# Router of the last batch with buffers of its own, and final statistics spread over two experts

## The reference

```python
x = layernorm(x + retention(x) + conv5(x))        # scan over tokens, one 512x512 product, 5 taps
x = layernorm(x + mlstm(q=x, k=ctx, v=ctx))       # 8 heads of 64, gates, decay matrix D:
#   C = (q k^T / 8) * D ;  h = C v / (max(|sum C|, exp(-m)) + 1e-6) ;  h = layernorm(h) * ln_scale
x = layernorm(x + moe(x))                         # 32 experts, top 2, capacity 160, 16 shared adapters
# moe: router input = [x, mean, std, min, max, l2, share of |x| < 1e-6]  (512 + 6 features)
#   h = gelu(input @ r1_w.T + r1_b) ; probs = softmax(h @ r2_w.T) ; the two best experts of a token
#   each expert takes its 160 best tokens: silu(gate) * up, then down, scattered back with weights
```

## Time and profile before

| | |
|---|---|
| Time of three runs | 1695.46 us median (1693.04 to 1701.02) |
| The profiled execution: its own time, its span | 1692.79 us, 1691.0 us |
| Busy share: TensorE, VectorE, ScalarE, GpSimd | 87%, 56%, 27%, 18% |
| Drain, from the last step's head work to `save` | about 528 to 605 us of the span |
| Selection, then the experts | from 605 us; expert 31 begins at 1638 us |

### The profile page before, as it was taken

How to read it: one execution, slowest core, us unless ns; L and a number is a source line. 1 busy time by engine, 2 the same in 40 slices (tenths; PEclk the granted TensorE clock), 3 DMA queues, 4 the chain that set the end, 5 groups by cost and what they waited for, 6 DMA issues and landing times.

```text
span 1691.0 us, 29270 instructions
## 1 busy us (share of the span) xinstructions
PE 1474.4 (87%) x10885; PEld 1132.8 (67%) x10921; DVE 953.3 (56%) x2778; ACT 463.0 (27%) x1111; POOL 309.3 (18%) x399
## 2 busy tenths in 40 slices
PE   5679998898898720499999999999999999999995
PEld 3356555555556410388887878888787888878784
DVE  8667999999987879624233242423324242332463
ACT  4556576676654510010010100001010010101023
POOL 4002121121111100111211212121121212112134
PEclk9689999999998755599999999999999999999998
DMA  6213213223210261056767677676777767677796
GB/s 174 69 31 89 75 63 113 64 74 83 80 51 1 100 277 59 16 184 238 290 218 293 243 278 269 234 292 219 288 248 270 277 229 293 219 293 249 267 348 197
DMA packets 92575, 311.03 MB, mean 184 GB/s; under 512 B 42838, under 2 KB 46940, under 8 KB 83164
## 3 DMA queue, kind: packets, MB, share of 16 engines
q1 hardware_dynamic: 79260, 287.87, 46.5%
q0 software_dynamic: 13248, 22.29, 5.8%
HBM read 273.18 MB, written 36.96 MB: 183 GB/s over the span
## 4 chain that ended last, share of the span: by engine, by line
PE 69%; DVE 22%; issue 5%; ACT 3%; POOL 1%; DMA 1%; DVEq 0%; POOLq 0%; ACTq 0%
PE bank L1003 37%; PE banks L1017 14%; PE bank L634 6%; PE banks L1020 4%; DVE arena L1405 3%; DVE arena L1836 2%; DVE arena L1395 2%; PE bank L636 1%; PE banks L731 1%; DVE arena L1567 1%; DVE arena L1576 1%; PE banks L712 1%; DVE arena L1426 1%; DVE arena L1445 1%; DVE arena L1893 1%
## 5 line engine op out<-in xcount | busy, mean ns | idle before, releaser
L1340 ACT ACTIVATE arena<-bank 128x160 f32<-128x160 f32 x288 | 87.1, 303 | 947.3 <-PE bank L1003 947.3
L1003 PE MATMUL bank<-keep,arena 128*128 128x160 f32 x2304 | 319.4, 299 | 2.4 <-DVE arena L2018 2.4
L1003 PE MATMUL bank<-arena 128*128 128x160 f32 x2304 | 320.1, 301 | 0.8 <-issue 0.8
L1003 PEld LDWEIGHTS bank<-keep,arena 128*128 128x128 f32 x2304 | 315.3, 189 | 5.8 <-issue 3.2
L1003 PEld LDWEIGHTS bank<-arena 128*128 128x128 f32 x2304 | 316.3, 191 | 4.2 <-issue 4.2
L2018 DVE TENSOR_TENSOR arena<-arena,bank 128x160 f32<-128x160 f32 x256 | 82.1, 321 | 405.6 <-ACT arena L1340 405.6
L1017 PE MATMUL banks<-arena 128*128 128x512 f32 x576 | 252.4, 592 | 0.0
L2203 POOL DMA_INDIRECT acc_rows<-arena,keep x64 | 102.8, 1606 | 625.6 <-DVE arena L1963 609.3
L1017 PEld LDWEIGHTS banks<-arena 128*128 128x128 f32 x576 | 107.6, 190 | 122.5 <-issue 122.5
L1961 DVE TENSOR_SCALAR arena<-banks,keep 128x512 f32<-128x512 f32 x32 | 24.0, 750 | 189.2 <-PE banks L1020 185.5
L634 PE MATMUL bank<-arena 128*128 128x512 f32 x224 | 107.8, 626 | 7.0 <-DVE arena L1405 7.0
(11 more groups left out here) (280 smaller groups left out, 1775.3 us busy)
## 6 DMA issues: line engine op xcount, KB each, us to landing
arena<-in_wup SPq DMA_DIRECT2D x32, 4096.0 KB, 12.4
arena<-in_wdn SPq DMA_DIRECT2D x32, 2048.0 KB, 9.4
arena<-in_aup SPq DMA_DIRECT2D x32, 512.0 KB, 11.5
arena<-in_xT SPq DMA_DIRECT2D x32, 256.0 KB, 2.8
arena<-in_kT SPq DMA_DIRECT2D x8, 1024.0 KB, 5.5
arena<-in_v SPq DMA_DIRECT2D x32, 256.0 KB, 6.3
x_rows<-arena SPq DMA_DIRECT2D x8, 1024.0 KB, 4.5
acc_rows<-arena SPq DMA_DIRECT2D x8, 1024.0 KB, 6.9
```

The costliest lines, as they stand in the source:

```text
L1003: m = pe.matmul(u[:, g * CAP:(g + 1) * CAP], w, xeT[e.slot][:, c, :], start=(c == 0), stop=(c == C - 1))
L1340: act.activation(sg[k], Ub[k][:, 0:CAP], ACT.Silu).then_inc(up_a(f"silu{j}"), 1)
```

## The change

Batch b gets its own buffers for sums and statistics. In the drain, its odd score tiles go to `Pp`, its even value tiles to `Sp`, and the order of several pieces moves on ScalarE, VectorE and TensorE. In the last two experts, VectorE's statistics are divided differently, and GpSimd's fourth `shifts` moves behind the scatter of expert 30.

```diff
+        rsum_l, rsq_l, nz_l, rvar_l, rt_l = (room.take(TB) for _ in range(5))
+        st6_l = room.take(TB, NSTAT)
+        def sums(b):
+            return (rsum_l, rsq_l, nz_l, rvar_l, rt_l, st6_l) if b.off == NB - 1 else (rsum, rsq, nz, rvar, rt, st6)
...
         def value_banks(b, j):
-            return Sp if b.off == NB - 1 and j % 2 else Pp
+            return Sp if b.off == NB - 1 and j % 2 == 0 else Pp
+        def score_banks(b, j):
+            return Pp if b.off == NB - 1 and j % 2 else Sp
...
             def scores(b, j):                                   # TensorE
+                if j == 1 and b.off == NB - 1:
+                    pe.wait_ge(*ev_v.at(f"out{NP - 1}", b - 1))
+                elif j and b.off == NB - 1:
+                    pe.wait_ge(*at_v.at(f"mul{j - 2}", b))
...
             def values(b, j):
-                if b.off == NB - 1 and j:
-                    pe.wait_ge(*(ev_v.at(f"out{j - 2}", b) if j > 1 else at_v.at(f"mul{NP - 1}", b)))
+                if b.off == NB - 1:
+                    pe.wait_ge(*(ev_v.at(f"out{j - 2}", b) if j > 1 else at_v.at(f"mul{j + 2}", b)))
...
                 last_router_rows(b)                             # TensorE, last_values
+                last_hidden(0)
                 router_stats(p, False)
                 router_hidden_stats(p)
-                last_hidden(0)
+                last_hidden(1)
                 router_logits(p)
-                last_hidden(1)
                 last_stats(b)
...
             def norm3_out(b):                                   # ScalarE; squares(b) alike
                 act.wait_ge(*l2_p.at("shift3", b))
-                act.wait_ge(*ro_v.at("stats", b - 1))
+                if b.off < NB - 1:
+                    act.wait_ge(*ro_v.at("stats", b - 1))
...
                 norm3_out(p)                                    # ScalarE, last_values
+                router_1(p, False)
                 squares(p)
-                router_1(p, False)
                 norm3_out(b)
                 last_copies(b)
+                squares(b)
                 router_stats(p)
-                squares(b)
                 table(ACT.Gelu, 1)
                 router_2(p, 0)
                 router_2(p, 1)
                 table(ACT.Exp, 2)
                 router_3(p)
+                last_stats()
                 router_4(p)
                 table(ACT.Gelu, 3)
-                last_stats()
                 last_gelu()
...
                 scale_queries(b, 0)                             # VectorE, last_values
-                norm2_stats(p)
                 weigh(b, 1)
...
                 scale_queries(b, 3)
+                norm2_stats(p)
+                head_out(b, 0)
                 norm2_scaled(p)
-                head_out(b, 0)
+                head_out(b, 1)
                 norm3_sum(p)
-                head_out(b, 1)
+                head_out(b, 2)
                 norm3_stats(p)
-                head_out(b, 2)
                 head_out(b, 3)
...
                 router_stats(p)
+                router_extreme(b, 0)
+                router_extreme(b, 1)
+                router_sparse(b)
+                router_stats(b)
                 softmax_2(p - 1)
                 top_two(p - 1)
-                router_extreme(b, 0)
-                router_extreme(b, 1)
                 softmax_1(p)
-                router_sparse(b)
-                router_stats(b)
                 softmax_2(p)
...
                     if last and j < J:                          # VectorE, expert
-                        statistics(2 * j + 16, 2)
+                        statistics(2 * j + 12 + min(j, 4), 3 if j < 4 else 2)
...
                 if isinstance(e.t, int) and e.off == NE - 2:
                     redone_rows()
-                    statistics(0, 16)
+                    statistics(0, 12)
...
-            for n in range(4):                                  # GpSimd
+            for n in range(3):
                 shifts(n)
             scatter_columns(next_last)
...
-            for n in range(4, 6):
+            for n in range(3, 6):
                 shifts(n)
```

More of the change, by code:

```diff
@@ L702, in scores @@
             def scores(b, j):
-                if j:
+                sp_ = score_banks(b, j)
+                if j == 1 and b.off == NB - 1:
+                    pe.wait_ge(*ev_v.at(f"out{NP - 1}", b - 1))
+                elif j and b.off == NB - 1:
+                    pe.wait_ge(*at_v.at(f"mul{j - 2}", b))
+                elif j:
                     pe.wait_ge(*at_v.at(f"mul{j - 1}", b))
@@ L711, in scores @@
                         half = slice(r * DH, (r + 1) * DH)
-                        m = pe.matmul(Sp[:, r * T + tb * P:r * T + (tb + 1) * P], kT[b.slot][half, j, rows],
+                        m = pe.matmul(sp_[:, r * T + tb * P:r * T + (tb + 1) * P], kT[b.slot][half, j, rows],
                                       qT[b.slot][half, j, rows], start=True, stop=True)
@@ L810, in last_stats @@
                 for tb in range(TB):
-                    m = pe.transpose(Bb[0:NSTAT, tb * P:(tb + 1) * P], st6[:, tb, :], ident)
+                    m = pe.transpose(Bb[0:NSTAT, tb * P:(tb + 1) * P], st6_l[:, tb, :], ident)
                 m.then_inc(rl_t("st"), 1)
@@ L1065, in norm3_out @@
                 act.wait_ge(*l2_p.at("shift3", b))
-                act.wait_ge(*ro_v.at("stats", b - 1))
+                if b.off < NB - 1:
+                    act.wait_ge(*ro_v.at("stats", b - 1))
                 for tb in range(TB):
                     act.activation(x2[b.slot][:, tb, :], x2[b.slot][:, tb, :], ACT.Identity, scale=rs3[:, tb:tb + 1],
-                                   bias=nb3[:, tb:tb + 1], accum_out=rsum[:, tb:tb + 1]).then_inc(n3_a(f"out{tb}"), 1)
+                                   bias=nb3[:, tb:tb + 1], accum_out=sums(b)[0][:, tb:tb + 1]).then_inc(n3_a(f"out{tb}"), 1)
             def squares(b):
                 act.wait_ge(*n3_a.at(f"out{TB - 1}", b))
-                act.wait_ge(*ro_p.at("l2", b - 1))
                 if b.off == NB - 1:
@@ L1076, in squares @@
                 else:
+                    act.wait_ge(*ro_p.at("l2", b - 1))
                     act.wait_ge(*ro_t.at("lg", b - 1))
-                act.wait_ge(*ro_v.at("stats", b - 1))
+                    act.wait_ge(*ro_v.at("stats", b - 1))
                 act.wait_ge(st_dum, 64)
@@ L1081, in squares @@
                     m = act.activation(square_rows(b, tb), x2[b.slot][:, tb, :], ACT.Square,
-                                       accum_out=rsq[:, tb:tb + 1])
+                                       accum_out=sums(b)[1][:, tb:tb + 1])
                 m.then_inc(n3_a("sq"), 1)
@@ L1425, in weigh @@
                 d = weights(b, j)
-                dve.scalar_tensor_tensor(d, Sp[:, :], DH ** -0.5, d, ALU.mult, ALU.mult).then_inc(at_v(f"mul{j}"), 1)
+                dve.scalar_tensor_tensor(d, score_banks(b, j)[:, :], DH ** -0.5, d, ALU.mult, ALU.mult).then_inc(at_v(f"mul{j}"), 1)
             def scale_queries(b, j):
@@ L1567, in router_sparse @@
                     m = dve.tensor_scalar(rows, rows, SPARSE_SQ, None, ALU.is_lt, ALU.add,
-                                          accum_out=nz[:, tb:tb + 1])
+                                          accum_out=sums(b)[2][:, tb:tb + 1])
                 m.then_inc(ro_v("cnt"), 1)
@@ L1574, in router_extreme, with router_stats @@
                     dve.wait_ge(*n3_a.at(f"out{TB - 1}", b))
-                    dve.wait_ge(*ro_t.at("st", b - 1))
-                dve.tensor_reduce(st6[:, :, 2 + k], x2[b.slot], AX.X, (ALU.min, ALU.max)[k]).then_inc(ro_v(f"extr{k}"), 1)
-            def router_stats(b):
-                dve.wait_ge(*n3_a.at("sq", b))
-                dve.wait_ge(*ro_p.at("l2", b - 1))
-                dve.wait_ge(*ro_t.at("st", b - 1))
+                    if b.off < NB - 1:
+                        dve.wait_ge(*ro_t.at("st", b - 1))
+                dve.tensor_reduce(sums(b)[5][:, :, 2 + k], x2[b.slot], AX.X, (ALU.min, ALU.max)[k]).then_inc(ro_v(f"extr{k}"), 1)
+            def router_stats(b):
+                rsum, rsq, nz, rvar, rt, st6 = sums(b)
+                dve.wait_ge(*n3_a.at("sq", b))
+                if b.off < NB - 1:
+                    dve.wait_ge(*ro_p.at("l2", b - 1))
+                    dve.wait_ge(*ro_t.at("st", b - 1))
                 dve.scalar_tensor_tensor(rt, rsum, 1.0 / (D * (D - 1.0)), rsum, ALU.mult, ALU.mult).then_inc(ro_v("msq"), 1)
```

## The result

The changed kernel took 1682.5 us (median of five runs, 1680.59 to 1683.51) where the kernel before took 1693.36 beside it: 10.9 us less by the medians. The ratio of the runs is 0.9924, 95% interval 0.9903 to 0.9946; it goes by all the runs and not by the medians, and one of the runs before took 1701.02 us. The profiled execution has a span of 1680.5 us, 10.5 less than before. Run once more later (`change_again`), the change took 1682.17, and its ratio was 0.9939 [0.9925, 0.9952].

The account below looks back on a forecast made before the run. VectorE was taken to bound the drain's second half, TensorE the experts. Gains of 8.7 (second half), 0.4 (first half) and 0.7 (end) sum to 9.8 us off 1692.8, 1683.0; plus 2.7 for the median gives 1685.7, range 1682.0 to 1690.5.

Parts of the forecast that it names:

- VectorE's list in the second half: Drain, second half: VectorE never starved, b's pieces directly behind p's, b's logits copied at N+35.2 instead of N+43.9.
- N: Start of `norm2_stats(b)` in the drain, 556.06 us before; forecast 1.8 us earlier to 1.0 later, taken as 0.4 earlier.
- cover for b's rows and squares: Drain, second half: b's rows ready at N+16.5, needed at N+18.5; squares by N+22, sparse count starting near N+23.
- The tables' drain: Rival: a table switch on ScalarE costs some 2.66 us, not 1.28, so main gain 7.3 us, time 1687.1; chance 0.05.
- p's logits: Third cover, drain's second half: p's logits ready at N+28, needed at N+29.5, slack 1.5 us.
- the fourth cover: Drain, second half: b's statistics ready N+25.7, roots N+28.1, GELU possible N+30.8, not before N+31.8 anyway: 1.0 us in hand.
- the main term: Drain, second half: b's logits copied at N+35.2 instead of N+43.9, a gain of 8.7 us.
- p's logits become the path: Rival: at 1.2 GHz the 5.5 us to p's logits double, 4.0 us lost after slack, time 1689.7; chance 0.12.
- The end: Experts 30 and 31: TensorE's stop shrinks by 1.2 us, three steps lose about 0.5; net gain 0.7, ends 0 and 1.2.
- moves all of that forward whole: From `save` to expert 30 nothing is edited, so the drain's saving was to reach the end undiminished; difference put at 0.
- TensorE-bound rival: Rival: TensorE stays at 1.2 GHz through the drain's second half, b's logits end at N+47.5, time 1698.4; chance 0.04.
- faster by over 0.5%: Whole kernel: chance 0.61 of a gain over half a per cent, that is below 1687.0 us.

Follow-up runs that it names:

- half_hidden: The change with half the chunks of both `last_hidden` left out, so b's router sees half its features: 1678.54 us, ratio 0.9915.
- split_hidden: The change with `last_hidden(1)` divided on TensorE, two chunks ahead of p's logits and two behind `last_stats(b)`: 1680.84 us, ratio 0.9931.
- first_half_old: The change with score and value tiles, their waits and VectorE's order in the drain's first half as before: 1683.24 us, ratio 0.9956.
- hidden_behind: The change with `last_hidden(1)` moved on TensorE from ahead of p's logits to behind `last_stats(b)`: 1681.67 us, ratio 0.9940.
- end_only: The kernel before with only the change's edits of the end (experts 30 and 31), the drain as before: 1692.04 us, ratio 1.0.
- table_first: The change with `last_stats` put behind the Gelu table load again on ScalarE: 1687.29 us, ratio 0.9965.
- split_six: `split_hidden` and `six_tiles` joined: 1680.93 us, ratio 0.9931.
- six_tiles: The change with ScalarE normalising 6 tiles between experts 30 and 31 in place of 8, the others one step later: 1680.74 us, ratio 0.9938.
- both: `hidden_behind` and `six_tiles` joined: 1681.74 us, ratio 0.9942.

## Why the prediction was right and wrong

**VectorE's list in the second half: right.** b's pieces followed p's at N+18.5 and ended at N+25.7, with each cover for b's rows and squares in place, and the table load cost its 1.28 us and no more (584.91 to 586.20, the dummy right behind it). The tables' drain had no part in it. With TensorE's work cut to the assumed length (`half_hidden`), the sum came out to 0.1 us.

**p's logits: the step that failed.** The prediction wrote "hidden statistics, `last_hidden(1)` and logits, 16 matrix products' time of about 0.45", so N+28, slack 1.5. The words and the sum don't agree: 16 times 0.45 is 7.2 us and would end at N+29.4 with no slack to speak of, while N+28 leaves room for 5.8 (the rival says 5.5), in which `last_hidden(1)` has 1.8. The row it rested on the earlier trace rows has 3.60 us for eight records, and I read it as the price of eight products, two `last_hidden`. It is one: each of its four chunks is two records. The code says four calls, the row says x8; the two were never set side by side. Both `last_hidden` are 7.2 us. The first held the transposes of p's statistics up to +22.3, though GpSimd's roots were done at +20.9, the second stood ahead of p's logits; these came at +30.7, and VectorE waited 1.54, the sign of being wrong that the prediction had named. For the same reason the fourth cover, "b's own statistics ... this 1.0 us holds", did not: b's transposes stood behind p's logits in TensorE's queue until +30.5 where the cover had them at +28.1. `half_hidden`, `split_hidden` and `first_half_old` carry this, all three with the clock whole up to b's logits: at the assumed length b's logits came at +35.3, divided at +35.8, whole at +36.55. It is worth 1.35 us. `hidden_behind` shows only that p's logits are then in time; b's came no earlier.

**The clock at the end of the drain: not in the sum.** I had it as part of a rival, priced on p's logits. It fell on b's hidden statistics, near 584.8 (by the 0.98 of the window up to 585), and cost 1.7 us (+38.28 against +36.55). Together with the 1.35 this is the 3.1 us by which the main term was too large. The rival "p's logits become the path" named the right wait and the wrong cause: the length of the queue, not the clock. No run shows what makes the clock fall there.

**N: the better end.** The range was 1.0 late to 1.8 early, and I took 0.4. It was 2.1 early: the clock stayed whole, in every trace with the new tiles, and the idle time was 0.55 and 0.61 (VectorE's rows after) in place of twice 1.79, with the new wait of 0.52. The argument that the change puts 0.6 us more of TensorE's work into the window before the fall was there, and was given no weight. With 1.83 us busy of 3 the clock stayed at 1.00, with 1.22 it fell. The Trainium skill (TensorE: Matmul & The Clock Gate, Part 1) has the array throttled by default and activity release it; these two traces agree. The fall at the end of the drain does not follow as easily: it came after 4.32 us busy of 5.

**The end: mechanism right, 0.7 forecast, 0.2 measured.** The stop was 1.26 us in place of 2.41, as computed from ScalarE's tiles. The three tiles a step cost the 0.5 us of the forecast, though not as stops: the 64 and 48 products behind the two stops took 9.28 and 6.83 us, where the pace of the earlier trace rows gives 8.9 and 6.7. The wait for `shifts(3)` was put at nothing, with "TensorE has half a step in hand"; ScalarE stood 2.57 us and TensorE 0.39. So 1.15 less 0.5 less 0.4 is the 0.2. GpSimd is the reason for the last term. It waits for the last load of the rows before it may scatter (2.82 us idle), and `shifts(3)` now stands behind that:

```profile
1636.20 1.68 POOL L2221 DMA_INDIRECT acc_rows<-arena,keep  x1 [2.82 <-issue]
```

In `split_hidden`, where expert 31 began earlier against these loads, the same stop was 1.28.

**The rest: put at nothing, and 2.5 us came.** The prediction wrote that what the drain saves "moves all of that forward whole". That step failed too: the stretch up to `mul0` was 1.1 us shorter, and that from `save` to expert 31 1.4. Neither is edited. The second goes with the clock at the start of expert 0 (last section), the first has no cause that a run shows.

**The sum: near by luck.** Against the forecast of 9.8 us the main term gave 3.0 less and the end 0.5 less, N 1.7 more and the unedited stretches 2.5 more; these errors cancel to the 10.5 us of the spans. Two of the announced signs came out by the same luck: b's logits were copied at 591.17 and `save` ended at 596.26, where 590.9 and 596.0 were forecast, though the second half was 3.1 us longer than the forecast had it. The median of 1682.5 is 3.2 under the forecast of 1685.7: 1.1 is the larger gain (10.9 by the medians), and 2.1 is that the forecast was built on a median of 1695.46 from three runs, where this comparison and later ones have 1691.4 to 1693.4 for the same kernel. It lies just inside the low end of the range, 1682.0; by the comparison's ratio, 0.9924, the gain is 12.9 of 1693.4 us and the time 1680.5, below the range. The range had taken in the bounds of each term, but no spread for the unedited 1600 us nor for the median it started from. Two smaller sums of the prediction are off as well, without consequence: the terms of the TensorE-bound rival add up to N+39.2 and not N+39.5, and those of "faster by over 0.5%" to 0.63 and not 0.61.

## What to carry to other kernels

Before a piece is costed from a row, set the count in the row (x8) beside the count in the code (four calls): float32 products came as two records each here, and a piece of four was as long as I had taken two pieces to be. When the order on one engine is improved, redo the queue of the engine that was idle before: from 564 us on TensorE had 7.1 us of waits, after the change 3.0, none of them ahead of p's logits. Where a kernel is as tight as this, the clock's fall is a term of its own, about as large as the edits: a piece that fills a wait on TensorE (`split_hidden`) gave 2.5 us in the drain, more than the queue alone accounts for, and 2.2 of them were gone again by the end of expert 31. And a range needs room for the stretches that nobody edits: here they moved by 2.5 us, a quarter of the gain.

## What the runs showed of the hardware

- **The drain's first half has two lengths, and the clock goes with them.** With the old tiles the granted clock was 0.50 to 0.58 from 531 to 534 us in the three traces, with the new ones 1.00 in all eleven; and `mul0` to N had only two lengths in fourteen traces, 27.1 and 25.0 to 25.1 us.
- **Where the clock comes back matters once more at expert 0.** `save` to its first product is 111.4 to 111.7 us in all traces, but to expert 31 it is 1031.8 to 1032.6 in some and 1033.2 to 1033.5 in others (before, `end_only`, `table_first`, `split_hidden`, `split_six`, `half_hidden`). Windows from expert 0's first product, first of the kernel before (it begins at 716.6), then of the change (at 707.7), then of `split_hidden` (at 704.6):

```profile
716.50:720.00 3.50, 3.37 (x13) 3.40 (x14) 0.03 (x1) 0.00 (x0) 0.00 (x0) 0.50 0.09 23
720.00:723.00 3.00, 3.00 (x14) 3.00 (x14) 0.32 (x1) 0.30 (x1) 0.00 (x0) 0.57 0.00 0
```

```profile
707.50:711.00 3.50, 3.31 (x12) 3.34 (x13) 0.09 (x1) 0.00 (x0) 0.00 (x0) 0.50 0.12 29
711.00:714.00 3.00, 3.00 (x23) 3.00 (x23) 0.32 (x1) 0.34 (x2) 0.00 (x0) 0.99 0.00 0
```

```profile
704.50:708.00 3.50, 3.36 (x13) 3.39 (x14) 0.03 (x1) 0.00 (x0) 0.00 (x0) 0.50 0.10 23
708.00:711.00 3.00, 3.00 (x15) 3.00 (x15) 0.32 (x1) 0.30 (x1) 0.00 (x0) 0.61 0.00 0
```

  In the change the second window is at 0.99, in the two others at 0.57 and 0.61. The first 144 products of expert 0 took 21.45 us in the change, 22.70 before and 22.59 in `split_hidden`, and the difference of 1.1 to 1.3 us is still there at expert 31. This is the 1.36 us of the table, and 1.3 of what `split_hidden` lost. No experiment moved it on purpose, so what decides it stays open.
- **The stretch before `mul0`** was 528.9 to 529.0 in the two traces without the drain's edits and 526.1 to 528.2 in the twelve with them. Half a us of it is there by the second step (71.65 before, 71.06 after, for the second batch's first product on VectorE), in code that the change does not touch. I have no cause for it.
- **An earlier scatter is not a faster one.** The last scatter of the rows took 3.4 us to land in the change and 4.9 in `six_tiles`, where it was issued 3.4 us sooner; in `both` and `split_six`, too, the work behind expert 31 was 21.7 us in place of 20.0.
